# Value products of chunk 3 ahead of chunk 0's transposes; the first forward unit of chunk 1 in two halves

## The reference

```
f1: RWKV attention: k, v, r = mixes of x and x shifted by a token, times Wk, Wv, Wr;
    a recurrence over time of (num, den, max) with decay per feature; f = (sigmoid(r) * wkv) @ Wo
f2: x and kernel rounded to fp8 (e4m3), product, bias in bfloat16
f3: x, z = W_in x; x = silu(causal convolution of 4 taps + conv_b)
    y = (long convolution of x with k_ssm, 512 taps, by FFT + D_skip * x) * silu(z);  f = W_out y
f4: mixture of 8 experts, 2 per token, and a shared one; two rounds of
    gelu(context @ w1) @ w2 -> alpha, beta, gate -> state update, then a refining layer with a halt gate
```

## Time and profile before

| what | us |
|---|---|
| median of 3 runs | 438.01 (437.89 to 438.79) |
| profiled execution, its own time | 440.64 |
| its span, first to last instruction | 438.5 |
| PE busy in it | 411.7 (94%) |
| DVE busy | 329.5 (75%) |
| ACT busy | 194.5 (44%) |
| POOL busy | 34.4 (8%) |

### The profile page before, as it was taken

The page is one execution under the profiler, slowest core; times in us unless marked ns, Lnnn a source line. Parts: engine busy times, 40 slices in busy tenths (PEclk is TensorE's granted clock), DMA queues, the critical chain, the costliest instruction groups (busy, mean ns, idle before and its releaser), DMA issues.

```text
span 438.5 us, 4421 instructions
## 1 busy us (share of the span) xinstructions
PE 411.7 (94%) x1507; PEld 214.1 (49%) x1507; DVE 329.5 (75%) x673; ACT 194.5 (44%) x321; POOL 34.4 (8%) x48
## 2 busy tenths in 40 slices
PE   7887898889999999999999999999999999999994
PEld 3344376577956384354544533334544433443362
DVE  4899989978764995979988798697635862374475
ACT  3355659543156413546154455253055626334432
POOL 1222424111000000000000000000000000000002
PEclk9898899989999999999999999999999999999998
DMA  7300000130000000000000000000000000000001
GB/s 243 128 1 1 1 0 1 17 140 1 0 1 0 2 0 0 0 1 1 1 1 0 0 1 24 1 0 1 0 0 1 25 1 0 1 0 0 1 0 48
DMA packets 4886, 7.10 MB, mean 16 GB/s; under 512 B 1031, under 2 KB 3713, under 8 KB 4737
## 3 DMA queue, kind: packets, MB, share of 16 engines
q1 hardware_dynamic: 4031, 4.92, 3.3%
q10 hardware_dynamic: 834, 1.91, 1.2%
HBM read 5.78 MB, written 1.05 MB: 16 GB/s over the span
## 4 chain that ended last, share of the span: by engine, by line
PE 70%; DVE 20%; ACT 4%; issue 2%; POOL 1%; DMA 1%; SPq 0%; POOLq 0%; DVEq 0%; ACTq 0%
PE ring L1379 22%; PE ring L1359 7%; PE bankA L198 5%; PE ring L1374 4%; PE ring L1361 3%; PE ring L1387 2%; DVE e2v L961 2%; PE ring L1401 2%; PE ring L1394 2%; PE ring L1405 2%; PE timebank L300 2%; PE bankA L300 2%; PE specbank L275 2%; PE bankA L275 2%; PE ring L1398 2%
## 5 line engine op out<-in xcount | busy, mean ns | idle before, releaser
L1379 PE MATMUL ring<-hm,wc 128*128 128x512 f32 (+1 forms) x252 | 108.6, 580 | 0.0
L1379 PEld LDWEIGHTS ring<-hm,wc 128*128 128x128 f32 x252 | 46.1, 190 | 61.0 <-issue 52.1
L1588 DVE SCALAR_TENSOR_TENSOR hm<-xtm,cst,h 128x512 f32<-128x512 bf16 x48 | 33.2, 745 | 2.8 <-ACT h L1493 2.8
L198 PE MATMUL bankA<-wconv,h2w 128*128 128x256 f32 x128 | 32.5, 401 | 0.0
L1507 ACT ACTIVATE gts<-ring 128x512 f32<-128x512 f32 (+1 forms) x18 | 9.9, 550 | 49.0 <-PE ring L1379 49.0
L1493 ACT ACTIVATE h<-ring,vec 128x512 f32<-128x512 f32 x32 | 21.8, 687 | 18.2 <-PE ring L1361 15.7
L198 PEld LDWEIGHTS bankA<-wconv,h2w 128*128 128x128 f32 x128 | 24.3, 199 | 4.8 <-issue 1.9
L1374 PE MATMUL ring<-hm,wc 64*128 64x512 f32 (+1 forms) x84 | 22.9, 621 | 1.2 <-DVE hm L1588 1.2
L1677 DVE SCALAR_TENSOR_TENSOR f2e<-hl,f2e 128x512 f32<-128x512 f32 (+1 forms) x9 | 5.7, 631 | 24.0 <-ACT hl L1538 23.9
L1359 PE MATMUL ring<-zs,wc 128*128 128x512 f32 x40 | 20.8, 602 | 0.8 <-DVE zs L1679 0.8
L1504 ACT ACT_TABLE_LOAD x8 | 10.3, 1283 | 25.3 <-PE ring L1379 25.3
(11 more groups left out here) (280 smaller groups left out, 813.1 us busy)
## 6 DMA issues: line engine op xcount, KB each, us to landing
wc<-in_w_c SPq DMA_DIRECT2D x1, 1664.0 KB
out<-xall SPq DMA_DIRECT2D x8, 128.0 KB, 1.9
cst<-in_const ACTq DMA_DIRECT2D x1, 838.5 KB, 8.9
wc<-in_x_feat SPq DMA_DIRECT2D x1, 768.0 KB, 9.8
wc<-in_k_time ACTq DMA_DIRECT2D x1, 512.0 KB
bconv<-in_bcast SPq DMA_DIRECT2D x1, 512.0 KB, 10.5
wc<-in_x_feat ACTq DMA_DIRECT2D x1, 256.0 KB, 4.1
wa<-in_w_a SPq DMA_DIRECT2D x1, 256.0 KB, 4.0
```

What stands on the lines that cost most here:

```text
L198: ins = pe.matmul(at, h2w[:, n, u % 2, u // 2:u // 2 + P], wconv[:, tap, :], start=False, stop=(h == HALVES - 1 and tap == TAPS - 1))
L1379: ins = pe.matmul(dst[:, at], wc[:, w:w + P], hm[:, seat(j, made + g - 1), at], start=False, stop=(g == PAIRS - 1))
L1588: dve.scalar_tensor_tensor(hm[:, seat(j, k), :], picked, cst[:, C_EG + g:C_EG + g + 1], h[:, g, :], ALU.is_equal, ALU.mult).then_inc(S["hm ...
```

## The change

Three places of the order change; no computation does.

- In pass 2 the value products of chunk 3 stand ahead of turn2(0); the receptance products of chunk 3 stay behind it. `project_value` takes the list of products to do.
- On ACT in pass 2, window(0) stands ahead of output_exps(2) and copy_key(3); passes 3 and 4 keep their order.
- In pass 4 the even half (e = 0) of forward_half(1, 0) stands between turn2(2) and the first piece of chunk 2. It waits for the first two pieces of chunk 1 (piece_kept at PIECES + BATCH = 6). The odd half (e = 1) stays at the end of the pass, with the wait for prod_done, and counts fwd_done.

```diff
--- before.py
+++ after.py
@@ -262,10 +262,10 @@
 
             return sum(BATCH for n in FOLDED if n < c) + b + 1
 
-        def forward_half(pe, c, b, bank, ahead=0):
+        def forward_half(pe, c, b, bank, ahead=0, evens=range(2)):
 
             after(pe, prod_done, 2 * c + b - ahead)
-            for e in range(2):
+            for e in evens:
                 for ri in range(2):
                     at = bank[:, e, ri * INNER:(ri + 1) * INNER]
                     if c in FOLDED:
@@ -273,7 +273,8 @@
                         continue
                     for par in range(2):
                         ins = pe.matmul(at, block_of(C_FWD, par, e, ri), xtm[:, c, b * HALVES + par, :], start=(par == 0), stop=(par == 1))
-            ins.then_inc(fwd_done, 1)
+            if 1 in evens:
+                ins.then_inc(fwd_done, 1)
 
         def keep_odd(act, c, b, bank):
 
@@ -673,11 +674,11 @@
                     if c > 0 and valid(c):
                         if c < CHUNKS - 1:
                             state_exps(c)
-                        else:
+                        if valid(c - 2):
                             window(c - 2)
                         output_exps(c)
                         copy_key(c + 1)
-                    if valid(c - 2) and c != CHUNKS - 1:
+                    if valid(c - 2) and c >= CHUNKS:
                         window(c - 2)
                     if valid(c - 1):
                         act.wait_ge(rstd1, c)
@@ -741,10 +742,10 @@
                     pe.matmul(psk[:, :], wmix[:, 0, 0, :], cur(hT, c), start=True, stop=False)
                     pe.matmul(psk[:, :], wmix[:, 1, 0, :], prev(hT, c), start=False, stop=True).then_inc(k_done, 1)
 
-                def project_value(c):
+                def project_value(c, kinds=((1, psv, v_done), (2, psr, r_done))):
 
                     after(pe, r_copied, c)
-                    for q, dst, done in ((1, psv, v_done), (2, psr, r_done)):
+                    for q, dst, done in kinds:
                         if c == 0:
                             pe.wait_ge(weights_mixed, 2 * q + 2)
                         pe.matmul(dst[:, :], wmix[:, 0, q, :], cur(hT, c), start=True, stop=False)
@@ -803,9 +804,14 @@
                             pe.wait_ge(r_copied, CHUNKS)
                             pe.wait_ge(piece_kept, BATCH)
                             forward_half(pe, 0, 0, pskv)
+                        if c == CHUNKS - 2:
+                            project_value(c + 1, ((1, psv, v_done),))
                         turn2(c - 2)
                         if c == CHUNKS - 2:
-                            project_value(c + 1)
+                            project_value(c + 1, ((2, psr, r_done),))
+                        if c == CHUNKS:
+                            pe.wait_ge(piece_kept, PIECES + BATCH)
+                            forward_half(pe, 1, 0, psro, 2, (0,))
                         piece(pe, c - 2, 0, 0)
                         turn1(c - 1)
                         piece(pe, c - 2, 0, 1)
@@ -822,7 +828,7 @@
                         piece(pe, c - 2, 2)
                         piece(pe, c - 2, 3)
                         if c == CHUNKS:
-                            forward_half(pe, 1, 0, psro, 1)
+                            forward_half(pe, 1, 0, psro, 1, (1,))
                     else:
                         inverse_half(pe, 0, 0, psf)
                         turn2(c - 2)
```

## The result

The changed kernel takes 436.40 us in the median of 8 runs (436.33 to 436.67), the kernel before beside it 438.40 (437.79 to 440.87, 8 runs). The ratio is 0.9949, 95% interval 0.9925 to 0.9973: faster by 0.5%, 2.0 us between the medians. Forecast were 433.9 us and 4.1 us, with a range from 432.8 to 436.0. The direction was right; the size was twice the measured one, and 436.4 lies above the range. Between the lowest executions of the two kernels, 437.79 and 436.33, lie 1.46 us.

The account below looks back on a forecast made before the run. The prediction took PE waits and half clock in passes 2 and 4 of the first stage as the bound. It summed 1.03 + 3.10 = 4.1 us, taking 438.01 to 433.9 us, range 432.8 to 436.0.

Parts of the forecast that it names:

- What bounds the kernel now: First stage, passes 2 and 4: PE waits, then runs at half clock (1.64 us in pass 4); DVE idles 1.03 and 1.48.
- steps 1 to 3: Pass 2: value products and window moved ahead at cost 0, ending DVE's wait; gain 1.03 us, bounds 0 and 2.4.
- step 4: Pass 4, behind the transposes: even half delays the first piece 0.27 us, but full clock brings turn1(3) 1.37 sooner.
- step 5: End of pass 4: only the odd half is left, 1.73 us less; with the earlier turn, 3.10 in all.
- the two lower bounds: Least gains: 0 us for pass 2; 1.46 for pass 4 if the clock falls all the same.
- Does the clock stay up?: Passes 2 and 4: clock stays full, argued from a lull at 40 to 42 us at 1.00; called the disputed term.
- pass 2 gives nothing: Pass 2: no gain, or a loss from a clock fall at the wait before lin(1); 434.9 or 435.5 us, chance 0.12.
- The first rival: Pass 4: the clock falls anyway, so pass 4 gives only 1.46 us; 435.5 us, chance 0.11.
- New falls behind the change: From pass 3 on: displaced waits meet clock falls costing 1.64 us each; 438.8 with three, 440.5 with four, chance 0.05.

Follow-up runs that it names:

- e1: The kernel before, run again with no edit: median 439.12 us, lowest 437.85, ratio to before 1.0017.
- e2: The kernel before with only the edits of pass 2 (value products and window ahead), forward unit (1, 0) whole: median 440.00 us, ratio 1.0024.
- e10: The kernel before with 11 in place of 9 warming matmuls at the start: median 440.22 us, ratio to before 1.0002.
- e5: The changed kernel, run again with no further edit: median 437.17 us, lowest 436.26, ratio to before 0.9948.
- e3: The kernel before with only the edit of pass 4 (even half moved ahead): median 436.86 us, ratio to before 0.9958.
- e11: The kernel before with only the edit of pass 4, and 11 in place of 9 warming matmuls: median 436.42 us, ratio to before 0.9916.
- e9: The changed kernel with 11 in place of 9 warming matmuls at the start: median 436.70 us, ratio to before 0.9931.
- e4: The kernel before with 8 idle matmuls between turn2(2) and the first piece of pass 4, no work moved: median 438.67 us, ratio 0.9999.
- e6: The kernel before with only the value products of chunk 3 ahead of turn2(0), ACT's order as before: median 439.20 us, ratio 1.0019.
- e7: The kernel before with 8 idle matmuls ahead of turn2(0) in pass 2 and 8 behind turn2(2) in pass 4: median 438.72 us, ratio 1.0007.
- e8: The changed kernel with 6 idle matmuls between turn2(1) and the first piece of pass 3: median 436.47 us, ratio to before 0.9948.

## Why the prediction was off, point by point

- **What bounds the kernel now**: read rightly from the profile, but taken for the kernel. This is the step that failed. The prediction took the two stretches of half clock, and the waits of DVE behind them, as part of every execution, and put 1.03 us for pass 2 and, for pass 4, 1.64 less the 0.27 of the later start into the sum. They were a property of the traced execution, where they cost 1.16 and 1.65 (against e1). Of 113 executions of before 54 lie within 0.5 us of the lowest, and e1's profile shows such a one without them: there the wait of pass 2 and the half clock of pass 4 are 0, and what is left of the 4.1 us is 1.46. The warning stood in the prediction itself: the profiled time was 2.6 us over the median, and it said that "nothing in the sum depends on that". These two terms did.
- **Value products and window (steps 1 to 3)**: each time of the timeline came as worked out, to 0.3 us, and against the profiled execution the 1.03 us of DVE's wait were won. Without the fall there is no such wait, and the part is worth 0. That is shown by e2 (lowest 437.91), by the lengths of e2 beside e10 and of e5 beside e3, and by pass 2 in the profile of e11. It was the lower bound of the part, and I took the 1.03 of the idle row.
- **Even half (step 4)**: 0.27 later start of the first piece, as forecast (e3). The 1.64 of half clock, which was to leave a net gain of 1.37, is only there in executions with the fall.
- **Odd half (step 5)**: 1.73, as forecast, measured as 1.45 net with the 0.27. So for an execution without a costly fall the sum is 0 + 1.45: 438.01 - 1.45 = 436.6, against 436.4 measured. This is the sum of the two lower bounds that the prediction wrote down (0 and 1.46).
- **Does the clock stay up?** In pass 4 of the changed kernel it does: its two profiles (the first and e5) have 1.00 from 84 to 108 us, and in the 20 executions of it, and the 12 of e3, none is over 2 us above its lowest, where 45 of 113 of before are, by 2 to 4.7 us. By this reckoning an execution that would have had the fall saves that much besides the 1.45, less up to about 1 us where a slow start is in it. Means tell this where medians don't: 439.28 for before (113 executions), 436.74 for the changed kernel (20), 2.5 us. I put it as gain of every execution. The argument for it did not hold: the empty stretch from 40 to 42 us, where the earlier trace rows have 1.00, is at 0.50 from 41 us on in e2, e9 and e10, where the PE waits 2.8 us before lin(0) and not 1.13. Nor had the clock fallen in two places only. The profile of before has two more falls, at 14 to 18 and 34 to 39 us, which cost nothing: the reciprocals of passes 1 and 2 start at 34.59 and 53.62, and at 34.61 and 53.63 in e1, which has neither.
- **The rivals**: *pass 2 gives nothing* was right for such executions, though not for its reason; there was no fall at lin(1). The first rival's number for pass 4, 1.46, was right, also for another reason: without the fall of pass 4 in either kernel (1.00 there in e1 and e5) that is what is left. *New falls behind the change*: a fall in pass 3 comes in the changed kernel's profile, and it is no property of the change, for e4 and e6 have it too (0.50 from 73 to 76 us in both). It is small, 0.36 us where 1.64 was reckoned (0.58 in e11 against e3), since DVE is in its reciprocal of pass 3 meanwhile (73.12 to 76.47) and then waits only 0.22 us (0.43 in e11).
- **Transposes and wait in pass 4**: the prediction noted for both falls that the PE's last work was transposes with pauses between them, with an idle wait in both. In e1 the transposes and the wait of pass 4 are those of the earlier trace rows (1.48 us and 1.40 us), and the clock is 1.00 behind them; in e2 and e10, with the same two lengths, it is 0.50. So the two together do not decide it. Nor are transposes needed for a fall. The first one in the profile of before (0.67 at 14 to 15 us, then 0.50) comes behind a wait of 1.91 us with only plain products ahead of it:

```profile
13.32 1.13 PE L741 MATMUL bankA<-wc,wmix 128*128 128x512 f32 x2 [1.91 <-DMA wc<-in_x_feat]
14.29 1.85 PE L742 MATMUL bankA<-wc,wmix 128*128 128x512 f32 x2
```

What stays open: whether the share of executions with a fall in pass 4 differs from job to job other than by chance (12 of the 23 runs of before in the last lie at 440.3 or more, 9 of the 35 in the first), what decides in one execution whether the clock falls, what a fall in pass 2 as first profiled costs over many executions (it was in no other of the profiles), and the three executions of e7 around 440.

## What to carry to other kernels

Compare the profiled execution's own time with the median of the runs before a term is read off it; where it is over by more than the runs' scatter, find which rows explain the excess and leave them out of what the edit can win in an ordinary execution. Here a stretch at half clock behind a wait of 1.4 to 1.5 us came in some executions and not in others, and filling the wait gained mostly in the spread and the mean of the times. Where there is work to put into such a wait, put the real thing there: the half unit brought 1.45 us also in executions without a fall. The idle matmuls of e4 took away the upper values and made the lowest executions 0.2 us slower (437.91 against 437.70).

## What was not expected of the hardware

- Behind the same 1.40 us wait in pass 4 the granted clock stayed at 1.00 (e1), was 0.50 for 3.4 us (before, 89.4 to 92.8; e6), or for 6.8 us (e2, 88.7 to 95.5; e10). From the reciprocal of pass 3 to the first gate that cost, against e1, 1.65 and 1.74 us in the shorter falls and 3.12 and 3.08 in the longer.
- A fall can cost nothing: e1, e3 and e5 have one at 42 to 46 us, while the output and key products run, and are among the lowest times of their kernels (437.85, 436.28, 436.40), for a wait behind it takes up the loss (in e1 the 1.54 us before the transposes of pass 2, which start at 47.32 and not 47.30). Where it lasted 6.8 us, from between 40 and 41 us on (e2, e9, e10), it cost 0.2 us: the reciprocals of passes 1 and 2 are 19.21 or 19.22 apart and not 19.02 or 19.03.
- The first products, after 9 idle matmuls, took the time of half clock until about 9.3 us in some executions (1.06 us a pair of 128x256 in e2 and e7) and that of full clock from about 6 us in others (0.59 in e1). With two more matmuls of warming no execution of e9 or e11 (17) is known to be of the slower kind, against 12 of the 32 of the changed kernel (first runs, e5 and e8) by their times.
